# Attention operands on one core of a Trainium2: the bf16 parts stored once in DRAM and loaded by pairs of products, in place of six products stored and loaded whole

## The chip, the cores and the metric

The kernel runs on one core of one Trainium2 chip. The metric is the time on the device in microseconds, the median of several executions. Three executions of the kernel before gave 1299.5, 1299.62 and 1301.71 us.

## The reference

Eight blocks run over one sequence of 2048 tokens of width 128, each with a layer norm before it and a residual after it: softmax attention, channel mix, gated linear attention, channel mix, retention, mixture of experts, lightning attention, mixture of experts. Only the first one matters here:

```python
def attention(x, W_qkv, q_scale, k_scale, W_out):          # 16 heads of 8, causal
    q, k, v = split(x @ W_qkv)
    q, k = layernorm(q) * q_scale, layernorm(k) * k_scale   # over all 128 channels
    s = einsum('bshd,bthd->bhst', q / sqrt(8), k)
    s = where(future, finfo.min, s)
    return einsum('bhst,bthd->bshd', softmax(s), v).reshape(B, S, D) @ W_out
```

## The kernel before

Tokens are handled in 4 chunks of 512. The scores are needed in float32, while the two operands of their matmuls are bf16. So each of q and k is split into three bf16 parts, high, mid and low, and the score is the sum of six products of parts (`PRODUCTS`: high·high, mid·high, low·high, high·mid, mid·mid, high·low). A head has 8 channels, so six products make 48 rows; three more rows (`extra`) hold the row maximum of q, split in the same way, against ones in k. These 51 rows (`KROWS`) are the contraction of every score matmul. Heads are paired: one of a pair has partitions 0 to 50 ("side" 0), the other partitions 64 to 114 (side 1). `Qs` and `Ks` are the resident stacks in SBUF, laid out [partition, pair, 2048 tokens] in bf16.

There are two blocks of code; no engine starts the second one before all are done with the first.

The first block loads x and all the weights on SP's queue (lines 387 to 404), normalises, projects to q, k, v, normalises q and k, turns them (line 546), and splits them into parts (`take_high`, `take_rest`, `take_mid`, `take_low`). The parts of a chunk are `parts[c]`, [128 partitions, q or k, 3 parts, 512 tokens]. A partition of it is (side, channel, pair), while a partition of the stack is (side, product, channel), with all eight pairs in it. So the parts pass through DRAM. `store(c)` (line 369) writes them with 12 DMAs into two DRAM tensors `q_stack` and `k_stack`, where each of the 6 products is written out in full, in rows of 1 KB. `stack(c)` (line 377) waits for `stored[c]` and loads Qs and Ks with 4 DMAs, each 48 partitions of one side, in pieces of 1 KB: first Q and K of side 0, then Q and K of side 1. SP runs `store(0)`, `stack(0)`, `store(1)` at the end of the first block, and `stack(1)`, `store(2)`, `stack(2)`, `store(3)`, `stack(3)` in the second.

The second block is the attention. It goes through 16 steps, each of one group of 4 heads and one chunk of queries: (group 0, chunk 0), (1, 0), (0, 1), (1, 1), (0, 2) and so on. For each step there are a pass for the row maxima (score matmuls at line 765, causal mask at 754 and 755, DVE's reduction at 714), then the maxima split by GpSimd (692 to 695), turned by TensorE (810), copied by DVE to `mrow` (727) and put into the rows 48 to 50 of Qs by four small DMAs, one for each head of the group (`set_maxima`, line 653: on ACT's queue for the first four steps, on SP's queue after them). Then come the transposed scores (782), exp on ACT (827), the causal cut on GpSimd (684), and the product with the values (796). All engines follow one order that `attention_order` plans beforehand. In that order the first maxima of step 2 (chunk 1) stand right behind those of step 1, and the first transposed scores of step 0 (`scores`, which wait for `max_set[j]`) right behind the first maxima matmul of step 2. The maxima of steps 2 and 3 need `stacked[1]`; chunk 2 is first needed by step 4, after all the maxima of step 3. After the attention each stage waits for the one before it.

Of the kernel before, what the change touches and what calls it, by code (L numbers as in the profile page):

```python
# [5 lines left out]
BF16 = mybir.dt.bfloat16  # L6
# [8 lines left out]
HD = D // H  # L15
P = 128
NT = T // P
CH = 512
NC = T // CH
# [6 lines left out]

ST = TOP * NT + E - 1
PARTS = 3
PRODUCTS = [(0, 0), (1, 0), (2, 0), (0, 1), (1, 1), (0, 2)]
PAIRS = H // 2  # L30
MROW = len(PRODUCTS) * HD
KROWS = MROW + PARTS
# [27 lines left out]
def build(nc, io):  # L60
    ctx = ExitStack()
    with ctx:
        def sb(name, shape, dt=FP32):
            return ctx.enter_context(nc.sbuf_tensor(name, shape, dt))
# [3 lines left out]
        def sem(name):  # L68

            stage_sems.append(nc.alloc_semaphore(name=name))  # L70
            return stage_sems[-1]
# [28 lines left out]
        arena = sb("arena", [P, 24 * 1024 + 8])  # L100
# [8 lines left out]
        left, right, table = cstb[:, 0:P], cstb[:, P:2 * P], cstb[:, 2 * P:320]  # L109


        stacks = [nc.dram_tensor(name, [NC, 2, MROW, PAIRS * CH], BF16, kind="Internal").ap() for name in ("q_stack", "k_stack")]

# [180 lines left out]
        def softmax_attention():  # L296

            QK = PAIRS * T // 2
            Qs, Ks = (arena[:, i * QK:(i + 1) * QK].bitcast(BF16).rearrange("p (n t) -> p n t", n=PAIRS) for i in (0, 1))
            at = 2 * QK  # L300
            room = [arena[:, at + i * 3 * CH:at + (i + 1) * 3 * CH] for i in (0, 1)]
            room += [w2[:].rearrange("p e f d -> p (e f d)")[:, i * 3 * CH:(i + 1) * 3 * CH] for i in (0, 1)]
            parts = [r.bitcast(BF16).rearrange("p (s r t) -> p s r t", s=2, r=PARTS) for r in room]
# [9 lines left out]
            with ExitStack() as mem:  # L313
# [40 lines left out]
                stored = [sem(f"a_stored{c}") for c in range(NC)]  # L354
                stacked = [sem(f"a_stacked{c}") for c in range(NC)]

                def store(sp, c):

                    row = PAIRS * CH
                    for s in (0, 1):  # L360
                        r = 0
                        for n in (3, 2, 1):
                            for side in (0, 1):
                                half = slice(side * P // 2, (side + 1) * P // 2)
                                if s == 0:
                                    src = parts[c][half, s, 0:n, :]
                                else:
                                    src = parts[c][half, s, 3 - n:4 - n, :].to_broadcast([P // 2, n, CH])
                                sp.dma_start(bass.AP(tensor=stacks[s].tensor, offset=((c * 2 + side) * MROW + r * HD) * row,
                                                     ap=[[CH, P // 2], [HD * row, n], [1, CH]]), src).then_inc(stored[c], 16)  # L370
                            r += n

                def stack(sp, c):
                    sp.wait_ge(stored[c], 16 * 12)
                    for side in (0, 1):
                        for dst, src in ((Qs, stacks[0]), (Ks, stacks[1])):
                            sp.dma_start(dst[64 * side:64 * side + MROW, :, c * CH:(c + 1) * CH],
                                         src[c, side].rearrange("r (n t) -> r n t", n=PAIRS)).then_inc(stacked[c], 16)

                def small_x(i, c):  # L380
                    return small[:, i, c * TPC:(c + 1) * TPC]
# [1 line left out]
                with nc.Block() as block:  # L383
                    @block.sync
                    def _(sp):
                        for c in range(NC):
                            sp.dma_start(x[:, c * TPC:(c + 1) * TPC, :],
                                         io["x"].rearrange("a (t p) d -> p (a t) d", p=P)[:, c * TPC:(c + 1) * TPC, :]).then_inc(x_loaded[c], 16)
                            if c == 0:
                                sp.dma_start(cst[:], io["cst"]).then_inc(tables_loaded, 16)  # L390
                                sp.dma_start(w["qkv"][:], io["qkv"]).then_inc(qkv_loaded, 16)
                        sp.dma_start(masks32[:], io["masks"]).then_inc(masks_loaded, 16)
                        for i, name in enumerate(("q_scale", "k_scale")):
                            sp.dma_start(scale[:, i:i + 1], io[name].rearrange("(n a) -> n a", a=1)).then_inc(scales_loaded, 16)
                        for i in (0, 1):
                            for side in (0, 1):
                                row = 64 * side + MROW
                                sp.dma_start(arena[row:row + PARTS, i * QK:(i + 1) * QK], io["extra"][i]).then_inc(extra_loaded, 16)
                        for name, _ in WEIGHTS[1:]:
                            sp.dma_start(w[name][:], io[name]).then_inc(loaded, 16)  # L400
                        sp.dma_start(w["lg2"][:], io["lg2"]).then_inc(loaded, 16)
                        sp.dma_start(out_bias[:], io["out_b"].rearrange("(a n) -> a n", a=1).to_broadcast([P, D])).then_inc(loaded, 16)
                        for i, name in enumerate(VECTORS):
                            sp.dma_start(vec[:, i:i + 1], io[name].rearrange("(n a) -> n a", a=1)).then_inc(loaded, 16)

                        sp.wait_ge(extra_loaded, 64)
                        for c in (0, 1):
                            sp.wait_ge(low, 2 * (c + 1))
                            store(sp, c)
                            if c == 0:  # L410
                                stack(sp, c)
# [236 lines left out]
                def set_maxima(eng, k):  # L648
                    g, c = STEPS[k]
                    eng.wait_ge(ring_read, RING["turn max", k] + 1)  # L650
                    for j in range(GH):
                        row = 64 * (j % 2) + MROW
                        eng.dma_start(Qs[row:row + PARTS, 2 * g + j // 2, c * CH:(c + 1) * CH],
                                      mrow[j * P // GH:j * P // GH + PARTS * TPC, :]).then_inc(max_set[j], 16)

                with nc.Block() as block:
                    @block.sync
                    def _(sp):
                        stack(sp, 1)
                        for c in (2, 3):  # L660
                            store(sp, c)
                            stack(sp, c)
                        for k in range(EARLY, NS):
                            set_maxima(sp, k)
                        for j in range(GH):
                            sp.wait_ge(max_set[j], 16 * NS)
                        sp.wait_ge(loaded, 16 * LOADS)
# [72 lines left out]
                    def _(pe):  # L740
                        def free_slot(what, n):

                            m = RING[what, n]
                            if m >= 2:
                                pe.wait_ge(ring_read, m - 1)
                            return RB + 2 * (m % 2)

                        def rows(stack, side, pair, a, z):
                            return stack[64 * side:64 * side + KROWS, pair, a:z]

                        def add_mask(side, out):

                            half = slice(64 * side, 64 * side + 64)
                            nc.tensor.matmul(out[:, 0:64], left[half], table[half], start=False, stop=False)
                            return nc.tensor.matmul(out[:, 64:P], right[half], table[half], start=False, stop=True)

                        def scores_for_max(n):

                            k, t, pl, kc, width = MAXIMA[n]
                            g, c = STEPS[k]  # L760
                            if n == m0[k]:
                                pe.wait_ge(stacked[c], 64)
                            bank = free_slot("max", n)
                            for side in (0, 1):
                                ins = nc.tensor.matmul(ps[:, bank + side, 0:width],  # L765
                                                       rows(Qs, side, 2 * g + pl, (c * TPC + t) * P, (c * TPC + t + 1) * P),
                                                       rows(Ks, side, 2 * g + pl, kc * CH, kc * CH + width), start=True, stop=kc < c)
                            if kc == c:
                                for side in (0, 1):
                                    ins = add_mask(side, ps[:, bank + side, width - P:width])  # L770
                            ins.then_inc(ring_ready, 1)
# [616 lines left out]
        def experts(name, token_rows, result_rows, last):  # L1388
# [54 lines left out]
            with nc.Block() as block:  # L1443
# [223 lines left out]
                def _(pe):  # L1667
# [37 lines left out]
                    for i in range(ST + 2):  # L1705
# [19 lines left out]
                        if s >= 0:  # L1725
# [6 lines left out]
                            ins.then_inc(down_ready, 1)  # L1732

        softmax_attention()
        channel_mix("f0")
        linear_attention("g", "gated")
# [77 lines left out]
```

## Time and profile before

| | |
|---|---|
| profiled execution, its own time | 1301.57 us |
| its span | 1299.8 us |
| TensorE matmul busy | 994.5 us |
| VectorE busy | 903.7 us |
| ScalarE busy | 508.2 us |
| GpSimd busy | 400.1 us |
| HBM read, written | 37.94 MB, 16.91 MB |
| packets of SP's DMA queue (q1) | 47480, 44.78 MB |

Busy time is the time in which an engine works on an instruction; DMA-issuing instructions are not in it. A DMA is issued by an engine's queue (SPq, ACTq) in about half a microsecond, and its data moves later on 16 DMA engines; a packet is one contiguous piece. In views of windows the DMA share can be over 1, because a packet's whole time is put down to the window in which it starts. The chain that ended last, as the page gives it, reaches back only to 1119 us and lies in the last mixture of experts, so it says nothing on the part that is changed; that part is at 28 to 100 us.

### The profile page before, as it was taken

The page shows a single profiled execution, that of the slowest core. Times are in us where ns is not written, and L with a number is a line of the kernel's source. Part 1 is how long each engine was busy: PE and PEld are TensorE (multiplying, and loading weights), DVE is VectorE, ACT ScalarE, POOL GpSimd, SP SyncE. Part 2 cuts the span into 40 slices and gives each one's busy share as a digit, 9 for nine tenths or more (in the row PEclk, how much of TensorE's full clock was granted, in tenths as well). Part 3 has the DMA queues.
Part 4 walks back from the last instruction along what each step waited for, and adds up shares of the span by engine and source line. Part 5 has one row for each costly group of instructions (what it writes and reads, how often), then busy time and mean ns, then how long its engine had stood idle before and what let it go on. Part 6 is the DMA issues. An engine that isn't in the chain of part 4 may idle for free. (4 is left out here: it accounts for less than half of the span.)

```text
span 1299.8 us, 17329 instructions
## 1 busy us (share of the span) xinstructions
PE 994.5 (77%) x5802; PEld 497.3 (38%) x5802; DVE 903.7 (70%) x1529; ACT 508.2 (39%) x1042; POOL 400.1 (31%) x479
## 2 busy tenths in 40 slices
PE   5477898999999998686667665399975775459994
PEld 3222222222222313444553213166652444336663
DVE  6957889898898700889977996633347997653335
ACT  5244566787778665321021001033334211113333
POOL 3211111011111112254434442156643444226662
PEclk9557789899999976789768985599997986669997
DMA  5890000000000001412101211011122120101114
GB/s 131 174 189 13 2 1 1 1 2 2 2 1 2 2 2 36 158 58 73 33 1 41 65 40 33 12 34 44 42 55 81 35 63 8 33 17 43 42 43 114
DMA packets 52797, 56.16 MB, mean 43 GB/s; under 512 B 7957, under 2 KB 40093, under 8 KB 52701
## 3 DMA queue, kind: packets, MB, share of 16 engines
q1 hardware_dynamic: 47480, 44.78, 13.5%
q0 software_dynamic: 4992, 10.23, 2.9%
q8 instruction: 50, 0.82, 0.3%
q14 instruction: 35, 0.28, 0.1%
q10 hardware_dynamic: 240, 0.05, 0.0%
HBM read 37.94 MB, written 16.91 MB: 42 GB/s over the span
## 5 line engine op out<-in xcount | busy, mean ns | idle before, releaser
L714 DVE TENSOR_REDUCE mpart<-ps 128x2 f32<-128x1024 f32 (+3 forms) x320 | 325.2, 1060 | 63.0 <-PE ps L765 38.3
L827 ACT ACTIVATE arena<-ps 128x512 f32<-128x512 f32 (+3 forms) x640 | 292.5, 541 | 155.1 <-PE ps L782 145.7
L782 PE MATMUL ps<-arena 51*128 51x512 bf16 (+3 forms) x640 | 187.5, 386 | 17.0 <-ACT arena L827 8.8
L1057 POOL TENSOR_TENSOR arena<-arena 128x512 f32<-128x512 f32 x96 | 122.2, 1273 | 165.1 <-DVE arena L1110 163.3
L796 PE MATMUL ps<-arena,w 128*32 128x512 f32 (+3 forms) x1280 | 168.9, 603 | 4.6 <-ACT arena L827 3.7
L765 PE MATMUL ps<-arena 51*128 51x512 bf16 (+3 forms) x640 | 152.0, 388 | 23.3 <-DVE mpart L714 15.3
L684 POOL TENSOR_SCALAR_AFFINE_SELECT arena<-arena 128x512 f32<-128x512 f32 x64 | 40.6, 635 | 325.8 <-ACT arena L827 254.3
L1559 DVE COPY arena<-ps 128x128 f32<-128x128 f32 x78 | 22.8, 292 | 161.7 <-PE ps L1702 161.7
L1649 ACT ACTIVATE arena<-ps 128x512 f32<-128x512 f32 x78 | 46.6, 597 | 218.9 <-PE ps L1712 218.9
L782 PEld LDWEIGHTS ps<-arena 51*128 51x128 bf16 x640 | 50.3, 96 | 186.7 <-ACT arena L827 146.4
L1096 DVE TENSOR_TENSOR arena<-arena 128x512 f32<-128x512 f32 x62 | 102.0, 1645 | 12.3 <-ACT arena L1163 4.6
L1614 POOL DMA_INDIRECT results<-arena x78 | 76.8, 984 | 90.5 <-DVE arena L1576 90.5
L1603 POOL DMA_INDIRECT arena<-tokens,arena x78 | 75.7, 970 | 76.9 <-DVE arena L1552 53.7
L1110 DVE TENSOR_TENSOR_SCAN arena<-cst,arena 128x512 f32<-128x512 f32 x64 | 87.4, 1366 | 0.0
L1711 PE MATMUL ps<-w,arena 128*128 x156 | 82.3, 610 | 2.9 <-DVE arena L1559 2.9
L1730 PE MATMUL ps<-w,arena 128*128 x624 | 82.7, 275 | 1.2 <-DVE arena L1576 1.2
L1712 PE MATMUL ps<-w,arena 128*128 x156 | 81.2, 603 | 0.0
L1730 PEld LDWEIGHTS ps<-w,arena 128*128 128x128 f32 x624 | 75.8, 192 | 1.6 <-issue 1.5
L182 PE MATMUL ps<-cst,xn 128*128 128x128 f32 x96 | 22.2, 393 | 60.5 <-DVE xn L165 58.7
L189 ACT COPY xt<-ps 128x512 f32<-128x512 f32 x28 | 16.2, 589 | 126.9 <-PE ps L182 126.9
L765 PEld LDWEIGHTS ps<-arena 51*128 51x128 bf16 x640 | 37.5, 97 | 69.3 <-DVE mpart L714 47.2
L1207 PE MATMUL ps<-arena 128*128 128x128 f32 x256 | 44.0, 326 | 25.9 <-POOL arena L1057 25.8
(261 smaller groups left out, 1479.6 us busy)
## 6 DMA issues: line engine op xcount, KB each, us to landing
w<-in_w SPq DMA_DIRECT2D x2, 2048.0 KB, 10.8
arena<-results SPq DMA_DIRECT2D x16, 256.0 KB, 5.1
arena<-g_v SPq DMA_DIRECT2D x15, 256.0 KB, 3.6
arena<-r_v SPq DMA_DIRECT2D x15, 256.0 KB, 3.6
arena<-l_v SPq DMA_DIRECT2D x15, 256.0 KB, 3.6
arena<-q_stack SPq DMA_DIRECT2D x8, 384.0 KB, 7.0
arena<-k_stack SPq DMA_DIRECT2D x8, 384.0 KB, 8.9
tokens<-arena SPq DMA_DIRECT2D x8, 256.0 KB, 2.4
```

The source lines that it names most:

```text
L714: nc.vector.tensor_reduce(out=mpart[:, 2 * pl:2 * pl + 2, t, kc], in_=ps[:, bank:bank + 2, 0:width], axis=AX.X, op=ALU.max).then_inc(ring_ ...
L765: ins = nc.tensor.matmul(ps[:, bank + side, 0:width], rows(Qs, side, 2 * g + pl, (c * TPC + t) * P, (c * TPC + t + 1) * P), rows(Ks, side, ...
L782: nc.tensor.matmul(ps[:, n % ST, off:CH], rows(Ks, j % 2, 2 * g + j // 2, kt * P, (kt + 1) * P), rows(Qs, j % 2, 2 * g + j // 2, c * CH + ...
L796: ins = nc.tensor.matmul(ps[32 * j:32 * j + 32, O, off:CH], vg[kt // (NT // 2)][:, kt % (NT // 2), g * GH + j, :], probs[:, u % 2, j, off: ...
L827: nc.scalar.activation(probs[:, n % 2, j[0], off:CH], ps[:, (GH * n + j[0]) % ST, off:CH], ACT.Exp, scale=float(HD) ** -0.5).then_inc(exp_ ...
L1057: nc.gpsimd.tensor_tensor(z[:, n % ZB, :], state[:, n % SB, :], q[:, c % 2, :], ALU.mult).then_inc(z_ready, 1)
L1096: nc.vector.tensor_tensor(upd[:, n % 2, :], v_in, k[:, n // HD % 2, :], ALU.mult).then_inc(upd_ready, 1)
L1110: nc.vector.tensor_tensor_scan(out=state[:, n % SB, :], data0=a, data1=upd[:, n % 2, :], initial=0.0 if c == 0 else state[:, (n - HD) % SB ...
L1614: nc.gpsimd.indirect_dma_start(out=result_rows, out_offset=bass.IndirectOffsetOnAxis(ap=result_row[:, s:s + 1], axis=0), in_=y[:, s % YB, ...
L1711: nc.tensor.matmul(ps[:, i % 2, :], xsT[:, i % 2, :], w1[:, expert[i], :], start=True, stop=True)
L1712: nc.tensor.matmul(ps[:, 2 + i % 2, :], xsT[:, i % 2, :], w3[:, expert[i], :], start=True, stop=True).then_inc(up_ready, 1)
L1730: ins = nc.tensor.matmul(ps[:, 7, 0:D], hidT[:, s % 2, f, :], w2[:, expert[s], f, :], start=f == 0, stop=f == NF - 1)
```

## The change

`store(c)` becomes one DMA: the three parts of q and k go to a DRAM tensor `sources` once each, 768 rows of 1 KB. `stack(c)` becomes 12 DMAs: for each pair of products (rows n and n+1 of `PRODUCTS`), each side, and each of Q and K, one DMA fills 16 partitions with 8 KB each. For that the products are put into another order (so that the two of a pair are a fixed distance apart in `sources`, which may be zero), and the resident stacks are laid out [partition, chunk, pair, 512 tokens], so that a partition's 8 pairs of a chunk are contiguous, in SBUF and in DRAM. The matmuls read the same values in rows as long as before.

```diff
-PRODUCTS = [(0, 0), (1, 0), (2, 0), (0, 1), (1, 1), (0, 2)]
+PRODUCTS = [(0, 0), (2, 0), (1, 0), (1, 1), (0, 1), (0, 2)]
...
-        stacks = [nc.dram_tensor(name, [NC, 2, MROW, PAIRS * CH], BF16, kind="Internal").ap() for name in ("q_stack", "k_stack")]
+        sources = nc.dram_tensor("sources", [NC, 2, PARTS, P, CH], BF16, kind="Internal").ap()
...
-            Qs, Ks = (arena[:, i * QK:(i + 1) * QK].bitcast(BF16).rearrange("p (n t) -> p n t", n=PAIRS) for i in (0, 1))
+            Qs, Ks = (arena[:, i * QK:(i + 1) * QK].bitcast(BF16).rearrange("p (c n t) -> p c n t", c=NC, n=PAIRS) for i in (0, 1))
...
                 def store(sp, c):
-                    row = PAIRS * CH
-                    for s in (0, 1):
-                        r = 0
-                        for n in (3, 2, 1):
-                            for side in (0, 1):
...
-                                sp.dma_start(bass.AP(tensor=stacks[s].tensor, offset=((c * 2 + side) * MROW + r * HD) * row,
-                                                     ap=[[CH, P // 2], [HD * row, n], [1, CH]]), src).then_inc(stored[c], 16)
-                            r += n
+                    sp.dma_start(sources[c].rearrange("s r p t -> p (s r) t"),
+                                 parts[c].rearrange("p s r t -> p (s r) t")).then_inc(stored[c], 16)
 
                 def stack(sp, c):
-                    sp.wait_ge(stored[c], 16 * 12)
-                    for side in (0, 1):
-                        for dst, src in ((Qs, stacks[0]), (Ks, stacks[1])):
-                            sp.dma_start(dst[64 * side:64 * side + MROW, :, c * CH:(c + 1) * CH],
-                                         src[c, side].rearrange("r (n t) -> r n t", n=PAIRS)).then_inc(stacked[c], 16)
+                    sp.wait_ge(stored[c], 16)
+                    for n in range(0, len(PRODUCTS), 2):
+                        for side in (0, 1):
+                            for s, stack_of in enumerate((Qs, Ks)):
+                                first, second = PRODUCTS[n][s], PRODUCTS[n + 1][s]
+                                row = 64 * side + n * HD
+                                at = ((c * 2 + s) * PARTS + first) * P * CH + side * P // 2 * CH
+                                sp.dma_start(stack_of[row:row + 2 * HD, c].rearrange("r n t -> r (n t)"),
+                                             bass.AP(tensor=sources.tensor, offset=at, ap=[[(second - first) * P * CH, 2], [PAIRS * CH, HD],
+                                                                                           [1, PAIRS * CH]])).then_inc(stacked[c], 16)
...
-                        eng.dma_start(Qs[row:row + PARTS, 2 * g + j // 2, c * CH:(c + 1) * CH],
+                        eng.dma_start(Qs[row:row + PARTS, c, 2 * g + j // 2, :],
...
-                            return stack[64 * side:64 * side + KROWS, pair, a:z]
+                            return stack[64 * side:64 * side + KROWS, a // CH, pair, a % CH:a % CH + z - a]
...
-                                pe.wait_ge(stacked[c], 64)
+                                pe.wait_ge(stacked[c], 16 * 12)
```

## Rows read from the trace of the kernel before

**Rows 1.** The page: busy time by engine, and TensorE's granted clock in 40 slices.
```profile
PE 994.5 (77%) x5802; PEld 497.3 (38%) x5802; DVE 903.7 (70%) x1529; ACT 508.2 (39%) x1042; POOL 400.1 (31%) x479
PEclk9557789899999976789768985599997986669997
```

**Rows 2.** The page: the costliest group, the reduction of the row maxima.
```profile
L714 DVE TENSOR_REDUCE mpart<-ps 128x2 f32<-128x1024 f32 (+3 forms) x320 | 325.2, 1060 | 63.0 <-PE ps L765 38.3
```

**Rows 3.** Windows (stretch: its length, busy time of five engines, PEclk, DMA share, GB/s).
```profile
140.00:460.00 320.00, 295.62 (x2383) 91.65 (x2379) 277.22 (x303) 230.85 (x491) 32.47 (x84) 0.94 0.01 2
```

**Rows 4.** Waits, 50 to 100 us (total, times, longest, in us).
```profile
PE ps L782 <- DMA arena<-mrow: 3.8, 2, 2.7
...
PE ps L765 <- DMA arena<-k_stack: 2.4, 1, 2.4
```

**Rows 5.** Timeline of PE (start, length, line, operation; in brackets the idle time before).
```profile
67.46 0.61 PE L765 MATMUL ps<-arena 51*128 51x512 bf16 x2 [2.40 <-DMA arena<-k_stack]
69.09 1.29 PE L782 MATMUL ps<-arena 51*128 51x512 bf16 x3 [1.02 <-DMA arena<-mrow]
...
84.76 1.21 PE L782 MATMUL ps<-arena 51*128 51x512 bf16 x3 [2.74 <-DMA arena<-mrow]
```

**Rows 6.** Timeline of SP's queue: stores (L369) and loads (L377) of the chunks.
```profile
28.98 3.99 SPq L369 DMA_DIRECT2D q_stack<-arena  x6
...
38.38 0.64 SPq L377 DMA_DIRECT2D arena<-q_stack  x1
...
41.05 3.89 SPq L369 DMA_DIRECT2D q_stack<-arena  x6
...
54.76 0.58 SPq L377 DMA_DIRECT2D arena<-q_stack  x1
...
71.45 0.58 SPq L377 DMA_DIRECT2D arena<-q_stack  x1
...
74.06 3.92 SPq L369 DMA_DIRECT2D q_stack<-w  x6
```

**Rows 7.** Windows around the transfers, columns as in rows 3.
```profile
4.00:8.00 4.00, 0.00 (x0) 0.00 (x0) 1.66 (x11) 0.59 (x2) 1.23 (x2) 1.00 1.04 341
...
39.50:50.00 10.50, 4.08 (x16) 2.99 (x16) 10.37 (x22) 4.48 (x7) 2.76 (x3) 0.50 1.05 158
50.50:54.00 3.50, 1.45 (x24) 1.04 (x24) 2.38 (x5) 0.40 (x1) 0.00 (x0) 0.50 1.07 370
57.00:66.00 9.00, 4.78 (x55) 2.42 (x51) 7.95 (x12) 0.00 (x0) 0.83 (x4) 0.50 1.12 165
...
75.00:83.50 8.50, 5.48 (x41) 1.76 (x40) 3.87 (x5) 2.14 (x8) 1.27 (x2) 0.50 1.11 151
...
516.00:523.00 7.00, 6.71 (x45) 6.30 (x43) 4.01 (x13) 2.35 (x4) 0.00 (x0) 0.77 0.97 335
```

**Rows 8.** Window of half a microsecond, halfway through the load of chunk 0.
```profile
45.00:45.50 0.50, 0.11 (x1) 0.00 (x0) 0.50 (x3) 0.35 (x1) 0.00 (x0) 0.50 1.06 211
```

**Rows 9.** DMA view: issue of the extra rows; then the packets of 9-10 and 18-20.5 us.
```profile
arena<-in_extra SPq DMA_DIRECT2D x4, 96.0 KB
...
DMA packets 403, 0.24 MB, mean 242 GB/s; under 512 B 163, under 2 KB 400, under 8 KB 400
...
DMA packets 470, 0.31 MB, mean 124 GB/s; under 512 B 55, under 2 KB 467, under 8 KB 467
```

**Rows 10.** Timeline of SP's queue: two issues that took ten times their usual 0.43 us.
```profile
11.73 4.64 SPq L400 DMA_DIRECT2D w_rq<-in_rq  x1
...
18.79 4.58 SPq L400 DMA_DIRECT2D w_lv<-in_lv  x1
```

**Rows 11.** Timeline of DVE: its last instruction of the first block.
```profile
50.16 1.46 DVE L488 TENSOR_TENSOR w<-arena,w 128x512 bf16<-128x512 f32 x2
```

**Rows 12.** Timeline of ACT's queue: the maxima of steps 0 and 1 sent to Qs.
```profile
62.77 3.90 ACTq L653 DMA_DIRECT2D arena<-mrow  x4
...
75.40 3.06 ACTq L653 DMA_DIRECT2D arena<-mrow  x4
```

More of the change, by code:

```diff
@@ L357, in store @@
                 def store(sp, c):
-                    row = PAIRS * CH
-                    for s in (0, 1):
-                        r = 0
-                        for n in (3, 2, 1):
-                            for side in (0, 1):
[L364 to L368, printed above, removed]
-                                sp.dma_start(bass.AP(tensor=stacks[s].tensor, offset=((c * 2 + side) * MROW + r * HD) * row,
-                                                     ap=[[CH, P // 2], [HD * row, n], [1, CH]]), src).then_inc(stored[c], 16)
-                            r += n
-                def stack(sp, c):
-                    sp.wait_ge(stored[c], 16 * 12)
-                    for side in (0, 1):
-                        for dst, src in ((Qs, stacks[0]), (Ks, stacks[1])):
-                            sp.dma_start(dst[64 * side:64 * side + MROW, :, c * CH:(c + 1) * CH],
-                                         src[c, side].rearrange("r (n t) -> r n t", n=PAIRS)).then_inc(stacked[c], 16)
+                    sp.dma_start(sources[c].rearrange("s r p t -> p (s r) t"),
+                                 parts[c].rearrange("p s r t -> p (s r) t")).then_inc(stored[c], 16)
+                def stack(sp, c):
+                    sp.wait_ge(stored[c], 16)
[8 more added lines that the diff above has]
+                                                                                           [1, PAIRS * CH]])).then_inc(stacked[c], 16)
                 def small_x(i, c):
```

## The prediction

> **What bounds the kernel now.** First the page's busy times [rows 1]: TensorE 994.5 us, VectorE 903.7 us of a span of 1299.8; the reader sees that neither is full all the time, and that the granted clock changes between its two levels, 1.2 and 2.4 GHz. The largest group is the reduction of the maxima, 320 times 1060 ns [rows 2]. The windows [rows 3] then show that from 140 us to the end of the attention TensorE is busy in 296 and VectorE in 277 of 320 us, with the DMA engines idle (share 0.01): this stretch is limited by computing, and in a fixed order. Nothing in it depends on a transfer of the chunks, so a delay or a gain at its start goes through to the end unchanged. The change can be worth only what transfers cost before 100 us. The waits there [rows 4] name two: 2.4 us for `k_stack`, and 3.8 us for `mrow`, the maxima on their way to Qs. The timeline of PE [rows 5] places them: at 67.46 the first maxima of chunk 1 start after the wait for the loaded stack; at 69.09 and at 84.76 the transposed scores of steps 0 and 1 start after waits for the maxima. These are the three places to work out. The last view is SP's queue [rows 6] beside the windows [rows 7].
>
> **How the transfers run before.** A chunk moves 1.57 MB out (12 stores) and 1.57 MB in (4 loads). The windows [rows 7] show two speeds: stretches with only stores go at 370 GB/s (50.5 to 54), stretches of loads at 151 to 165 (75 to 83.5 with hardly anything else: 151). So a load takes 1.57 / 0.151 = 10.4 us, and a store 4.3. The load of chunk 1 is issued at 54.76 [rows 6] and PE goes on at 67.46 [rows 5]: 12.7 us, so 2.3 us besides the data, of which I put 1.4 ahead of the first byte and 0.9 behind the last.
>
> The small DMAs of the maxima behave as if they stood in one line with everything SP has issued. The first of step 1 is issued at 75.40 [rows 12]; SP had by then issued the whole load of chunk 2 (from 71.45) and two stores (from 74.06) [rows 6]. That load's data ends at about 83.5 (71.45 + 1.4 + 10.4), and the maxima land at 84.76. Those of step 0, issued from 62.77, land at 69.09, when nearly all of the stores of chunk 2 are through. So their landing is set by the end of the data ahead of them.
>
> **What the change does to one store.** 12 issues (7.9 us from 28.98; SP goes on at 38.38, so 9.4 us in all [rows 6]) become one of some 0.6 us with 0.79 MB: 2.1 us at 370 GB/s, and 1.5 us around it as before: 4.2 us. The sure part is -5.2 us on each store that is waited for.
>
> **What it does to one load.** The bytes stay 1.57 MB; 4 issues become 12, at 0.62 us each 7.4 us, which hides behind the data unless that goes faster than 210 GB/s. The open cost is the speed. Row length explains nothing: 128 partitions get 341 GB/s at 4 to 8 us, where most rows are the 512 B of x, and 335 at 516 us with 2 KB rows [rows 7]; 1 KB stores get 370. What is different in the slow loads is that 48 neighbouring partitions of one side are written. The other case of few partitions is `in_extra`: 4 DMAs of 96 KB, each 3 partitions, sides in turn. The views [rows 9] show 3 packets of 8 KB or more starting at 9 to 10 us and again at 18 to 20.5 (four such triples in all, one a DMA), and SP's second long issue ends at 23.37 [rows 10]. 393 KB in 14.2 us is 27.7 GB/s, although the sides alternate. So 3 partitions get 28, 48 get 151, 128 get 340. The new loads write 16. Between 3 and 48 lie four doublings for 123 GB/s, 31 each; 16 is 2.4 doublings up: 102 GB/s. Against that, the speed rises for half a microsecond where the load passes from side 0 to side 1 (211 GB/s [rows 8]); the new order passes five times in place of one. 5 x 0.5 us at some 160 (0.4 MB) and the rest, 1.17 MB, at 102 make 2.5 + 11.5 = 14.0 us; I take 14.2. Bounds: 85 GB/s (18.5 us, towards a straight line between the two rows, which gives 63) and 210 (7.5 us, the issue).
> The Trainium skill (SBUF — State Buffer, Door 1: The DMA port swizzle) says that the partition number picks one of 16 ports: 16 neighbours reach 4 of them, 48 reach 8 with half of these carrying double. By its 27.2 GB/s a port the new loads get an estimated 109 GB/s, 14.4 us, and the sum below would be +3.3 in place of +3. By that rule 48 partitions would get 163 (the trace has 151), and 3 would get 27.2 (the trace has 27.7).
>
> **The sum, in order of time.** Chunk 0: store issued 28.98 as before (SP sends weights until then), landed 33.1; load issued 33.1, data 34.5 to 48.7 (before: to 50.2). Nothing is gained at the start of the attention: VectorE's last instruction of the first block ends at 51.62 [rows 11], and all wait for that; the stack of chunk 0 has landed 2 us before. Store 1 is issued at about 40.5, behind the load; its data is through at 50.8. So SP issues stack 1 at 51.9, when the block starts, not at 54.76: 2.9 us earlier. It takes 14.2 + 2.3 = 16.5 us: 68.4 against 67.46, **+0.9** (-2.9 + 3.8). Store 2 follows: data to 69.5. The maxima of step 0 have only it ahead: about 69.9 against 69.09, **+0.8** in all; ACT's four issues took 3.90 us beside SP's and 3.06 the next time [rows 12]; that 0.8 us gains nothing, since landing decides. SP sees store 2 landed at 69.8 (before 71.45) and issues stack 2: data 71.2 to 85.4, then store 3, issued at 77.2, to 87.5. The maxima of step 1 are issued from 76.2 to 79.3: the first has the load ahead and lands at 86, the other three have store 3 ahead too and land at 88. Against 84.76 that is +1.2 to +3.2; the first three are used at once, so **+3**. Load 3, issued at 88, is through by 104, before the maxima of step 2 are needed: nothing more. The matmuls read rows of the same length in the new layout, and the order of products costs nothing. After that there is no cover left to lose.
> Profiled: 1301.57 + 3 = 1304.6. The median of the runs shown lies 2 us under the profiled execution, so for the median 1299.6 + 3 = **1302.6**.
>
> **Rivals.**
> A rate per DMA engine. The 3 partitions of the extra rows may have used three DMA engines, 9.2 GB/s each; the 48 partitions used all 16, 151 / 16 = 9.4 each. If that is the limit for few partitions, or if the engines drift apart so that both sides are in use, 16 partitions get about 150 GB/s and a load stays at 10.4. Then stack 1 lands at 51.9 + 12.7 = 64.6: the wait of 2.4 us is gone; maxima of step 0 at 66.3 (-2.8); stack 2 issued at 66.3, data to 78.1, maxima of step 1 at 80.5: -4.2, **1295.4**. For it: the two equal quotients. Against it: 128 partitions give each engine 21, also with rows of one partition.
> Long rows are fast. Loads run as fast as they are issued, 210 GB/s: all three waits go, 3.6 us at the first two together and 2.7 us at the third: -6.3, **1293.3**. Against it: row length shows no effect in [rows 7]. The Trainium skill (Perfetto Trace Analysis, DMA Optimizations) has this rule, from 2 KB to 4 or 8 KB a great gain; no load of this trace bears it out.
> The two cancel: load of 12.3 to 13.5 us (117 to 128 GB/s, six passes between sides helping more than I allowed): stack 1 within 1 us of before, maxima of step 1 at 83.5 to 86: -1.3 to +1, **1299.6**.
> Slower on the other side of my forecast's range: the limit is sharper, as at 25 GB/s for the busiest sixth of a 48-partition load (151 / 6); four such make 100, or down to 85: load 15.7 to 18.5 us. Stack 1 lands at 70 to 73 (+2.6 to +5.5), stack 2's data ends at 88.5 to 94: +5.5 to +9, **1306**. It decides from 113 GB/s downwards: above that the earlier issue wins, below it the slower load.
>
> **Chances.** My forecast, slower loads at 102 to 113 GB/s, +1 to +4.5 us: 0.38. Sharper limit: 0.12. Cancel: 0.19. Rate per engine or drift: 0.24. Long rows: 0.07. What spreads each case further is the clock: it stays at 1.2 GHz through the transfers (0.50 [rows 7]) and is at 0.94 of full speed on the mean after 140 us [rows 3], so a shift of a few us can move the rise, which I put at one or two us either way. What can be told from no change is 0.2%, 2.6 us. Slower by more: two thirds of the forecast, all of the sharper limit, 0.02 of the cancelling: 0.39. Faster by more: 0.24 x 0.85, the long rows, and 0.03 of the cancelling: 0.30. The rest, 0.31, within. The range with 8 in 10: 1294.4 to 1306.6; the forecast's own is 1300.5 to 1304.5.
>
> **What would show it.** One SP issue at 28.98, the first of 12 loads at about 33; loads in windows without stores at 100 to 113 GB/s with DMA share at or over 1; stack 1 issued at 51.9 (sure: else SP was held up) and PE's first wait for `stacked` ending at 68 to 69; the scores of step 1 starting at 87 to 88. If the window of a load shows 150 or more, the forecast is wrong in its main term, and the end comes 4 us earlier than before; if PE waits less and the end is still not earlier, the clock or the order of the attention took it back.

## The result and the profile after

| | median | executions | span of the profiled one |
|---|---|---|---|
| before | 1300.61 us | 1299.5 to 1301.71 | 1299.8 us |
| after | 1333.96 us | 1328.55 to 1335.49 | 1326.8 us (its own time 1328.55) |

The ratio is 1.0243, with a 95% interval of 1.0206 to 1.0279: 2.4% slower. One further execution of the changed kernel took 1854 us, at a granted clock of 1.0; it is left out of the range and the ratio but not of the median, which is 1332.43 us without it, and nothing here explains it. The forecast was 1302.6 us, its range ended at 1306.6.

The page of the kernel after, for [rows 1] and [rows 2], and its list of waits from 30 to 200 us, for [rows 4]:

```profile
PE 989.6 (75%) x5802; PEld 497.5 (37%) x5802; DVE 904.1 (68%) x1529; ACT 508.6 (38%) x1042; POOL 400.2 (30%) x479
...
L709 DVE TENSOR_REDUCE mpart<-ps 128x2 f32<-128x1024 f32 (+3 forms) x320 | 325.2, 1060 | 93.9 <-PE ps L760 58.7
```
```profile
PE ps L760 <- DMA arena<-sources: 38.0, 2, 21.8
...
PE ps L777 <- DMA arena<-mrow: 3.2, 4, 1.2
```

The work is the same: 5802 matmuls, VectorE at 904.1 us against 903.7. (TensorE's 989.6 against 994.5 us goes with a higher granted clock at the end of the attention, below.) What has grown is waiting. PE waited 2.4 us for the stacks, now 38.0 in two pieces. PE's timeline, first in the kernel before, where the attention starts, then in the kernel after, against [rows 5] too:

```profile
51.94 0.29 PE L765 MATMUL ps<-arena 51*128 51x128 bf16 x2 [3.20 <-PEq L383]
```

```profile
64.64 0.29 PE L760 MATMUL ps<-arena 51*128 51x128 bf16 x2 [16.21 <-DMA arena<-sources]
...
99.60 0.60 PE L760 MATMUL ps<-arena 51*128 51x512 bf16 x2 [21.82 <-DMA arena<-sources]
100.00 1.06 PE L777 MATMUL ps<-arena 51*128 51x512 bf16 x3
...
115.07 0.60 PE L777 MATMUL ps<-arena 51*128 51x512 bf16 x1 [0.71 <-DMA arena<-mrow]
```

The attention starts at 64.6 us where it started at 51.9, and chunk 1 comes at 99.6 where it came at 67.5: +12.7, then +32.1 (both are differences of the rows shown). SP's queue, against [rows 6]:

```profile
28.56 0.38 SPq L359 DMA_DIRECT2D sources<-arena  x1
32.20 9.24 SPq L371 DMA_DIRECT2D arena<-sources  x12
41.48 2.08 SPq L359 DMA_DIRECT2D sources<-arena  x1
66.66 7.60 SPq L371 DMA_DIRECT2D arena<-sources  x12
```

The store is as short as hoped: 3.6 us from its issue to the first load. The load is not: issued at 32.20, it releases PE at 64.64. The windows give the reason, against [rows 7] (the last two columns are the DMA share and GB/s):

```profile
44.00:46.00 2.00, 0.81 (x4) 0.40 (x2) 2.00 (x8) 1.19 (x2) 0.00 (x0) 0.50 1.01 369
...
52.00:64.00 12.00, 0.00 (x0) 0.00 (x0) 0.00 (x0) 0.00 (x0) 0.00 (x0) 0.50 0.13 55
64.00:66.60 2.60, 1.44 (x24) 1.01 (x24) 1.24 (x3) 0.00 (x0) 0.00 (x0) 0.50 0.11 38
...
82.00:98.00 16.00, 0.00 (x0) 0.00 (x0) 0.00 (x0) 0.00 (x0) 0.00 (x0) 0.50 0.13 53
```

Loads go at 53 GB/s with a DMA share of 0.13, which is 2 engines of 16, each at 26.5. The share tells this from the limit that was forecast: with all engines held up at the destination it would be near 1, as it was before at 151 GB/s. In the windows from 52 and from 82 us no compute engine does anything. The store of chunk 1, issued behind the load, moves at 369 GB/s in the middle of it (44 to 46 us), as 14 engines would be free for it. SP sees it landed only at 66.66, 2 us behind the load: from 64.0 to 66.6 another 0.1 MB goes at 38 GB/s, which is 2/16 of the store's 0.79 MB. It fits that the two slow engines' part of the store came last; the windows do not name the engines.

From step 5 on the lag is constant. The copy of the maxima of step 5, and the one of the last step, in the kernel before and then in the kernel after (DVE's timeline):

```profile
189.56 0.21 DVE L727 COPY mrow<-ps 128x128 bf16<-128x128 bf16 x1
...
456.98 0.22 DVE L727 COPY mrow<-ps 128x128 bf16<-128x128 bf16 x1
```
```profile
219.76 0.21 DVE L722 COPY mrow<-ps 128x128 bf16<-128x128 bf16 x1
...
487.35 0.22 DVE L722 COPY mrow<-ps 128x128 bf16<-128x128 bf16 x1
```

+30.2 and +30.4 us. The span grew by 27.0; the other 3.4 came back at the end of the attention, where the granted clock was higher (last section).

### The profile page after: what moved, and what is told of

It is laid out like the page before. It is cut to its first block and busy times, and to the rows that moved or that the text cites. A ratio compares the mean times of both kernels' runs of the same rounds, so it can differ in the third digit from the quotient of the medians.

```text
span 1326.8 us, 17317 instructions
## 1 busy us (share of the span) xinstructions
PE 989.6 (75%) x5802; PEld 497.5 (37%) x5802; DVE 904.1 (68%) x1529; ACT 508.6 (38%) x1042; POOL 400.2 (30%) x479
## 5 line engine op out<-in xcount | busy, mean ns | idle before, releaser
L791 PE MATMUL ps<-arena,w 128*32 128x512 f32 (+3 forms) x1280 | 164.4, 588 | 5.0 <-ACT arena L822 4.0
```

Of the source, the lines that this page charges most:

```text
L791: ins = nc.tensor.matmul(ps[32 * j:32 * j + 32, O, off:CH], vg[kt // (NT // 2)][:, kt % (NT // 2), g * GH + j, :], probs[:, u % 2, j, off: ...
```

## The experiments

Theory E: a load runs on as many DMA engines as the outermost dimension of its DRAM side has entries; the change made that 2. Rival Z: 8 KB rows, the repeated reading of the same parts, or the single store are slow. Theory P is the prediction's: writing few neighbouring partitions limits a load. Theory L: the maxima's small DMAs stand in line behind the data issued before them. The labels that begin with e test the first three, those with v test L and loads over 128 partitions. All ratios are to the kernel before, run beside them.

**e1_channel_outer**: the changed kernel, channels outermost.

```diff
-    bass.AP(tensor=sources.tensor, offset=at, ap=[[(second - first) * P * CH, 2], [PAIRS * CH, HD], [1, PAIRS * CH]])
+    bass.AP(tensor=sources.tensor, offset=at, ap=[[PAIRS * CH, HD], [(second - first) * P * CH, 2], [1, PAIRS * CH]])
```

> The changed kernel, with one edit: in the 12 loads of a chunk the DRAM side's pattern has the 8 channels outermost and the 2 products inside, in place of 2 products outermost (the rows of a pair lie in the stack in another order, the same in Q and K). Bytes, rows of 8 KB, destinations and number of issues are the same. Theory E (a load runs only on as many DMA engines as the outermost dimension of its DRAM side has entries: 2 in the changed kernel, whose loads go at 53 GB/s with a DMA share of 0.13; here 8): the share rises to about 0.5, the speed at least twofold. If nothing else limits, 8 x 26.5 = 210 GB/s, a load of 7.5 us, and all waits for transfers go: 1294 us. Theory E with the prediction's limit for 16 neighbouring partitions (102 to 110 GB/s): a load of 14.2 to 15.5 us, 1302 to 1306 us. Rival Z (rows of 8 KB, or parts read again from the same DRAM rows, are slow by themselves): 53 GB/s and 1332 us as in the changed kernel.

Measured: 1299.32 us against 1299.51, ratio 0.9993 (0.997 to 1.0016). The whole loss is gone by the order of two dimensions. The time is 3 us under what was expected of E with a limit for 16 partitions. The loads themselves took what the prediction gave them: PE goes on with chunk 1 16.5 us after the issue at 52.27.

```profile
52.31 0.29 PE L760 MATMUL ps<-arena 51*128 51x128 bf16 x2 [3.20 <-PEq L378]
...
68.76 0.61 PE L760 MATMUL ps<-arena 51*128 51x512 bf16 x2 [3.34 <-DMA arena<-sources]
...
82.48 0.61 PE L777 MATMUL ps<-arena 51*128 51x512 bf16 x1 [0.18 <-DMA arena<-mrow]
```

A window with nothing but the load of chunk 2 on the DMA engines:

```profile
72.00:79.00 7.00, 5.47 (x34) 1.47 (x31) 3.23 (x5) 2.18 (x6) 2.02 (x6) 0.66 0.51 118
```

Share 0.51: 8 engines, 118 GB/s, not 8 x 26.5 = 212. Z falls, since the rows, the repeated reading and the single store are all still there, and a second limit shows.

**e2_one_product**: one product, 8 partitions, in each load.

```diff
-    for n in range(0, len(PRODUCTS), 2):
+    for n in range(len(PRODUCTS)):
...
-    sp.dma_start(stack_of[row:row + 2 * HD, c]..., ap=[[(second - first) * P * CH, 2], [PAIRS * CH, HD], [1, PAIRS * CH]])
+    sp.dma_start(stack_of[row:row + HD, c]..., ap=[[PAIRS * CH, HD], [1, PAIRS * CH]])
```

> The changed kernel with each load taking one product in place of two: 24 loads a chunk, each 8 partitions of 8 KB, the DRAM side's outermost dimension 8 (the channels). Theory E alone: 8 DMA engines, up to 210 GB/s, so limited by 24 issues of 0.62 us, 15 us a chunk: 1302 to 1306 us, windows of loads at about 105 GB/s. Theory E with the limit by neighbouring partitions (27 GB/s for each four of them): 8 partitions get 50 to 55 GB/s although 8 engines work, share about 0.5 with little moved, a load of 29 us: 1330 us, as slow as the changed kernel. Rival Z: 53 GB/s and 1332 us too, but with a DMA share near 0.13.

Measured: 1334.05 us, ratio 1.0252 (1.0198 to 1.0305). The window shows the second limit alone:

```profile
72.00:82.00 10.00, 0.00 (x0) 0.00 (x0) 0.96 (x2) 0.00 (x0) 0.00 (x0) 0.50 0.53 66
```

Share 0.53, so 8 engines as in e1, but 66 GB/s on 8 partitions where e1 has 118 on 16. As slow as the change, for another reason; the share tells the two apart. (PE waits 24.4 us for stacks here and another 20.4 us for maxima.)

**e3_rows_8k_48**: the kernel before with only the new layout, so 4 loads of 48 rows of 8 KB.

```diff
-    sp.dma_start(dst[64 * side:64 * side + MROW, :, c * CH:(c + 1) * CH], src[c, side].rearrange("r (n t) -> r n t", n=PAIRS))
+    sp.dma_start(dst[64 * side:64 * side + MROW, c].rearrange("r n t -> r (n t)"), src[c, side])
```

> The kernel before (12 stores of all six products, 4 loads of 48 partitions), with only the new layout of the resident stacks, so that each load moves rows of 8 KB in place of 1 KB on 16 DMA engines. Theory of the prediction (few neighbouring partitions limit, row length doesn't): loads at 150 to 165 GB/s as before, 1299.6 us within 1.5. Rival, long rows are fast: loads at 210 GB/s or more, 7.5 us or less, all waits for transfers go: 1293 to 1295 us.

Measured: 1300.01 us, ratio 0.9981 (0.9952 to 1.001).

```profile
41.00:49.00 8.00, 4.08 (x16) 3.00 (x16) 7.94 (x21) 3.91 (x6) 0.83 (x1) 0.50 1.01 148
```

148 GB/s; before it is 153 in the same window. Rows of 8 KB bring nothing.

**e4_16_rows_16_engines**: e3 with 12 loads of 16 rows that lie one after another in DRAM.

```diff
-    for side in (0, 1):
+    for n in range(0, MROW, 16):
+        for side in (0, 1):
...
-            sp.dma_start(dst[64 * side:64 * side + MROW, c]..., src[c, side])
+                sp.dma_start(dst[64 * side + n:64 * side + n + 16, c]..., src[c, side, n:n + 16])
```

> The kernel before with its 12 stores and DRAM stacks, the new layout of the resident stacks, and 12 loads of 16 partitions x 8 KB a chunk: the shape and destinations of the changed kernel's loads, but each reads 16 rows one after another in DRAM (outermost dimension 16). Theory E with the prediction's limit for 16 partitions: 102 to 110 GB/s with all 16 engines busy (share about 1), a load of 14.4 to 15.4 us in place of 10.4; the attention starts 3.6 us later, the maxima of step 1 land some 12 us later: 1309 to 1314 us. Theory E alone: 16 engines, limited by the issue at 210 GB/s: 1294 to 1297 us.

Measured: 1305.32 us, ratio 1.004 (1.0018 to 1.0062), 4 us under the expected range: a load ran at 120 and not at 106, and the attention started at 52.5 us and not 3.6 us late.

```profile
40.00:50.00 10.00, 4.08 (x16) 3.00 (x16) 9.87 (x22) 4.24 (x7) 2.52 (x2) 0.50 1.04 120
```

16 engines are busy (1.04) and move 120 GB/s, as 8 did in e1 with 118. On 16 partitions the number of engines beyond 8 doesn't matter.

**e5_outer_2** and **e6_outer_4**: e3, the load's 48 rows written as 2 x 24, and as 4 x 12.

```diff
-    src[c, side]
+    bass.AP(tensor=src.tensor, offset=(c * 2 + side) * MROW * PAIRS * CH,
+            ap=[[MROW // 2 * PAIRS * CH, 2], [PAIRS * CH, MROW // 2], [1, PAIRS * CH]])
```

> The kernel of e3_rows_8k_48 (12 stores of all products, 4 loads of 48 partitions x 8 KB), with the DRAM side of each load written as 2 x 24 rows in place of 48 rows: the same bytes from the same addresses to the same partitions. Theory E (engines = outermost dimension of the DRAM side): 2 engines, DMA share 0.13, 53 GB/s, a load of 30 us in place of 10.4, as in the changed kernel; the attention starts at about 70 us and waits again for chunk 1: 1333 to 1345 us. Rival (the single store, the repeated reading of parts, or 16-partition pieces made the changed kernel slow): loads at 150 GB/s, 1300 us.

> As e5_outer_2, with 4 x 12 rows. Theory E: 4 engines, DMA share 0.25, 4 x 26.5 = 106 GB/s, a load of 14.8 us; the attention starts about 4 us later and waits more for chunk 1 and the maxima, near e4_16_rows_16_engines: 1304 to 1312 us. Rival: 150 GB/s, 1300 us.

Measured: 1299.96 and 1293.31 us, ratios 0.9997 (0.9962 to 1.0033) and 0.9977 (0.9938 to 1.0016); their loads ran at about 150 GB/s with shares near 1 (e5 152 GB/s at 0.99 from 41 to 49 us, e6 151 at 0.98 from 76 to 82). Both expectations missed: the dimensions lie end to end in memory, so the pattern names one run of rows, and it was treated as one. They tested nothing of E, and led to e7.

**e7_outer_2_gap**: e5 with an unused row between the halves in DRAM, which the stores skip.

```diff
-    [NC, 2, MROW, PAIRS * CH]
+    [NC, 2, MROW + 2, PAIRS * CH]
...
-    ap=[[MROW // 2 * PAIRS * CH, 2], ...]
+    ap=[[(MROW // 2 + 1) * PAIRS * CH, 2], ...]
```

> The kernel of e3_rows_8k_48 with one unused row left in the DRAM stacks between rows 23 and 24 of each side, so that the DRAM side of a load is 2 x 24 rows that can't be merged into 48. (In e5 and e6 the two dimensions lay end to end, and the windows show 16 engines still working: the form was merged, so they tested nothing.) Same bytes, partitions, rows of 8 KB and number of DMAs. Theory E: 2 engines, share 0.13, 53 GB/s, 30 us a load: the attention starts near 70 us and waits again for chunk 1: 1333 to 1345 us. Rival (single store, repeated reading or 16-row pieces made the changed kernel slow): 150 GB/s, 1300 us.

Measured: 1341.91 us, ratio 1.0325 (1.0274 to 1.0376). PE's timeline:

```profile
70.88 0.29 PE L766 MATMUL ps<-arena 51*128 51x128 bf16 x2 [22.21 <-PEq L384]
...
106.77 0.61 PE L766 MATMUL ps<-arena 51*128 51x512 bf16 x2 [22.77 <-DMA arena<-k_stack]
```

And a window early in the load of chunk 0:

```profile
42.00:44.00 2.00, 1.09 (x5) 0.79 (x6) 2.00 (x9) 0.00 (x0) 0.20 (x1) 0.50 0.14 57
```

Share 0.14 at 57 GB/s, two engines again; later windows also hold pieces of the store. The load of chunk 0 is issued at 37.15, so PE starts 33.7 us after it, as in the change (32.4). (SP needs 21 us for the six issues of stores behind that load, where it needed 3.9 [rows 6].) The attention starts at 70.9, as expected. The stores are those of before but for the skipped row, each row of DRAM is read once, and the loads have 48 partitions: besides the rows of 8 KB, which e3 cleared, the one thing shared with the change is the outermost 2. With e1, which takes it away, and e7, which brings it alone, E is shown for 2.

**v3_before_gated**: the kernel before with waits on SP, so that the maxima have nothing ahead of them.

```diff
-    for c in (2, 3):
-        store(sp, c)
-        stack(sp, c)
+    sp.wait_ge(max_set[GH - 1], 16)
+    store(sp, 2)
+    sp.wait_ge(max_set[GH - 1], 32)
+    stack(sp, 2)
+    store(sp, 3)
+    sp.wait_ge(max_set[GH - 1], 48)
+    stack(sp, 3)
```

> The kernel before with only the order on SP changed: the store of chunk 2 is issued after the maxima of step 0 have landed, the load of chunk 2 and the store of chunk 3 after those of step 1, the load of chunk 3 after those of step 2. Theory L (the small DMAs of the maxima land only when the data issued ahead of them is through): PE goes on at 67.5 with the maxima of chunk 1 as before, the scores of step 0 start at about 67.9 in place of 69.1, those of step 1 without a wait, 4 us earlier in all: 1295 to 1296.5 us. Rival (the maxima take their time by themselves, or the order of the attention gives the time back): within 1 us of before, with the wait at the scores of step 1 still there.

Measured: 1295.47 us against 1300.08, ratio 0.9969 (0.9942 to 0.9997). From 50 to 100 us PE has 2.9 us of waits for stacks, as before, and none for the maxima; only a weight load waits 0.3 us for them:

```profile
PE ps L769 <- DMA arena<-k_stack: 2.9, 1, 2.9
PEld ps L786 <- DMA arena<-mrow: 0.3, 1, 0.3
```

L holds: 3.8 us of waits [rows 4] were only a place in line. The trace says it more firmly than the ratio, whose interval nearly reaches 1: at the last copy of the maxima the kernel is at 453.05 us where before it is at 456.98, 3.9 earlier.

**v4_channel_outer_gated**: e1 with the same order on SP.

> The kernel of e1_channel_outer (parts stored once, loads of 16 partitions on 8 DMA engines) with the same order on SP as v3_before_gated. Theory L: the stack of chunk 1 lands at 68.8 as in e1, the scores of step 0 start at 69.2, those of step 1 without the waits of 1.2 us in all: 1297 to 1298.5 us, 1 to 2 us under e1. If the single store is worth more than the slower load when nothing stands in line, it comes near v3_before_gated (1295.5).

Measured: 1297.53 us, ratio 0.998 (0.9959 to 1.0001): as expected, and not distinguishable from before, nor from v3, whose median is 2 us lower. That the single store makes up for 16-partition loads is not shown, and neither is the opposite.

**v2_loads_128**: e3 with DRAM stacks of 64 rows a side, filled once at the start in rows 48 to 63, and one load for all 128 partitions of Q and one for K.

```diff
-    for side in (0, 1):
-        for dst, src in ((Qs, stacks[0]), (Ks, stacks[1])):
-            sp.dma_start(dst[64 * side:64 * side + MROW, c].rearrange("r n t -> r (n t)"), src[c, side])
+    for dst, src in ((Qs, stacks[0]), (Ks, stacks[1])):
+        sp.dma_start(dst[:, c].rearrange("r n t -> r (n t)"), src[c].rearrange("a r m -> (a r) m"))
```

> The kernel before with 12 stores, the new layout of the resident stacks, and DRAM stacks of 64 rows a side, whose rows 48 to 63 are filled once at the start (zeros for q, ones for k), so that a chunk is loaded with 2 DMAs over all 128 partitions, 8 KB each. A load moves 2.1 MB in place of 1.57. Theory P (the speed of a load goes by the partitions it writes): 340 to 375 GB/s, 5.7 us of data; the stack of chunk 1 is issued at 51.9, landed at 60, and its wait goes; the maxima of step 0 stand behind the load of chunk 2 and land at 69 to 70 as before; those of step 1 at 80.5, before they are needed: 1296.5 to 1298 us. Rival (a load of the stacks is limited to 150 GB/s by something else, such as DRAM pages or 16 rows of 8 KB in flight): 14 us of data, slower than before, 1302 to 1306 us.

Measured: 1300.61 us, ratio 0.9994 (0.9967 to 1.002), 3 us over the expectation. Its loads are fast, but the fill and the extra rows hold SP up at the start, which I had left out:

```profile
37.07 3.96 SPq L370 DMA_DIRECT2D q_stack<-arena  x6
```
```profile
57.50 0.29 PE L767 MATMUL ps<-arena 51*128 51x128 bf16 x2 [8.60 <-PEq L382]
```

The first store is issued 8 us later than before (28.98 [rows 6]), and the attention starts at 57.5, 5.6 us late. What the loads gave, the start took.

**v6_loads_128_no_extra**: v2 without the four loads of the extra rows into SBUF (they come with the chunks).

```diff
-    for side in (0, 1):
-        row = 64 * side + MROW
-        sp.dma_start(arena[row:row + PARTS, i * QK:(i + 1) * QK], io["extra"][i])
```

> The kernel of v1_loads_128_gated with the order on SP of the kernel before (no wait for the maxima): it parts what the fast loads bring from what the order brings, and differs from v2_loads_128 only by the extra rows that are no longer loaded into SBUF (in v2 they and the fill of the DRAM rows held SP up, and the attention began at 57.5 us). Theories P and L: attention begins at 51.6 as in v1, no wait for the stack of chunk 1, the maxima of step 0 stand behind the load of chunk 2 and land at 68 to 69.5, those of step 1 behind chunk 3's data: 1294 to 1297 us, 2 to 4 us above v1. If the order is worth nothing once loads are fast: equal to v1.

Measured: 1296.26 us against 1300.24, ratio 0.9965 (0.9935 to 0.9995). **v1_loads_128_gated** is the same with `sp.wait_ge(max_set[GH - 1], 32)` ahead of the load of chunk 2.

> The kernel of v2_loads_128 without the loads of the extra rows into SBUF (they come with the chunks), and with the load of chunk 2, the store and the load of chunk 3 issued after the maxima of step 1 have landed. Theories P and L together: all three waits for transfers before 100 us go (2.4, then 1.2 and 2.7, and what hangs on them): the scores of step 0 start at about 65.9, those of step 1 at 78.5: 6 us earlier, 1293 to 1295 us. If the attention gives some back by waits among the engines: 1295 to 1297.

Measured: 1289.83 us against 1300.08, ratio 0.9949 (0.9919 to 0.9979), the lowest of all, and 3 us under the expectation. Its executions lie at 1286 to 1290 (six) and 1294 to 1297 us (five), so the 10 us between the medians overstate the gain. PE in v6, then the load of chunk 3 and PE's wait for maxima in v1:

```profile
70.50 0.60 PE L780 MATMUL ps<-arena 51*128 51x512 bf16 x2 [3.24 <-DMA arena<-mrow]
```
```profile
90.00:95.00 5.00, 2.34 (x19) 1.00 (x15) 4.61 (x8) 0.58 (x1) 0.83 (x4) 0.74 0.98 403
...
PE ps L782 <- DMA arena<-mrow: 0.2, 1, 0.2
```

The stacks of 128 partitions load at 403 GB/s, and no wait for a stack is left. v6 still has 3.2 us for maxima behind the load of chunk 2; in v1 the order takes it away. The intervals of the two ratios overlap, so the difference is read from the last copy of the maxima, first in v6, then in v1 (before: 456.98):

```profile
453.36 0.22 DVE L725 COPY mrow<-ps 128x128 bf16<-128x128 bf16 x1
```
```profile
450.64 0.22 DVE L727 COPY mrow<-ps 128x128 bf16<-128x128 bf16 x1
```

The fast loads are 3.6 us ahead of before, the order adds 2.7: 6.3 in all, as expected. The profiled execution of v1 is 14 us shorter than that of before; the other 7.5 us come in the stretch up to the load of `w1`, where its granted clock was higher (last section).

## Why the prediction was wrong

**What bounds the kernel; where a delay goes: right but for the clock.** The lag came through the attention nearly unchanged, 30.2 to 30.4 us over the last 268 us of it. Not all went through to the end: 3.4 us came back at the end of the attention, by the clock; the prediction allowed the clock "one or two us either way" for a shift of a few us.

**One store: right.** 3.6 us from issue to SP going on, against 4.2.

**One load: wrong, and this is the step that failed.** The term was "I take 14.2" us, at 102 GB/s, with a lower bound of 85 GB/s (18.5 us). I read the speed of a load from the partitions it writes and took for granted that all 16 DMA engines carry it, also where I wrote the rivals. The new loads' DRAM side is [2 products][8 channels][8 KB], so each runs on two engines: 53 GB/s, 29.7 us, twice the term. The sign that the prediction named, a DMA share at or over 1 in windows of loads, came out at 0.13. There was a hint beforehand, no more: `in_extra`, with 3 rows a DMA, had three long packets a DMA, so at most three engines carried each. I used it for the speed and named "three DMA engines" only in a rival, without asking what number the new loads would have. The Trainium skill has the rule (DMA: Bandwidth & Descriptors, Why a DMA increments its semaphore by 16 and not by 1): the number of engines is the largest up to 16 that divides the slowest dimension larger than 1 of both sides. For the change that gives 2, for e1 and e2 8, for e3 and e4 16, for e7 2; the shares of 0.13, 0.51 and 0.53, 1.01 and 1.04, and 0.14 agree with it.

**The sum around that term: right where it is put in.** With 29.7 in place of 14.2 the timetable gives chunk 0 at 32.2 + 2.3 + 29.7 = 64.2 (measured 64.64) and chunk 1 at 66.66 + 32.0 = 98.7 (99.60); 32.2 and 66.66 are the measured issues. Its line "Nothing is gained at the start of the attention" named 2 us of cover but no risk: the load of chunk 0 moved that start by 12.7 us.

**The forecast's mechanism, tried without that fault (e1): right in the load, wrong in the last term.** Loads of 16 partitions are slower than those of 48: 118 to 120 GB/s against 148 to 153. The estimate by doublings (102) was 14 to 15% under these windows, but the time was right: predicted for stack 1 were the issue at 51.9 and PE going on at 68.4, e1 has 52.27 and 68.76. The +3 us came from the maxima of step 1, which were to land at 86 to 88; in e1 PE takes them at 82.48 to 84.75, before was 84.76. They are issued at 75.96, when SP is 5.5 us into the 8.66 us that its 12 issues of that load take, so they would have only about two thirds of the load ahead of them, not all of it. Without that term earlier issue and slower load cancel, as the ratio of 0.9993 shows: the rival's time, though stack 1 came as in the forecast.

**The rivals.** "Long rows are fast" is refuted by e3. "A rate per DMA engine" of 9.4 GB/s is refuted by the change, where an engine moves 26.5, and by e2: 8 engines move 66 GB/s on 8 partitions and 118 on 16 (e1).

**The line of small DMAs: right** (v3, and v1 against v6).

## What to carry to other kernels

Before a DMA is reshaped, read both its patterns from the outside: the outermost dimension that doesn't merge with the next set the number of engines here, and in the windows the DMA share tells it (0.13 is two). Then ask how many partitions it writes, and divide the speed by the busy engines: in the change it was 26.5 GB/s an engine, and more engines helped; at 15 (e1), 8 (e2) or 9 (before) the engines were held up by something else, here the few partitions, whatever the share. And small transfers that someone waits for should be issued before the large ones that nobody needs yet; that order alone was worth 0.3% here (v3, 3.9 us by its trace).

## What the runs showed of the hardware

Speed of a load by the partitions of one DMA, with the engines at work:

| partitions | engines | GB/s | from |
|---|---|---|---|
| 8 | 8 | 66 | e2 |
| 16 | 8 and 16 | 118, 120 | e1, e4 |
| 48 | 16 | 148 to 153 | e3, before |
| 128 | 16 | 403 | v1 |

Each figure is one window with hardly anything but loads; other such windows give 62 to 76 in e2, 114 to 121 in e1 and 113 to 115 in e4. The size of a DMA grows with its partitions here (64, 128, 384 KB and 1 MB), and no run holds one and varies the other; against the size alone speaks `in_extra`, 96 KB a DMA on 3 partitions at the prediction's 27.7 GB/s. By the ports of the Trainium skill (SBUF — State Buffer, Door 1: The DMA port swizzle) an estimate gives 54, 109 and 163 for the first three rows; the order agrees, while the windows shown are 21% and 8 to 10% above it and then 6 to 9% below it. Stores read 64 partitions of one side at a time and yet reach 370 GB/s [rows 7]; the limit of the loads does not show in them.

The granted clock at the end of the attention differs between executions. e3 and e6 move the same bytes in the same way (e6's pattern was merged), yet the profiled ones have spans of 1299.4 and 1291.7 us. The same stretch, first in e3, then in e6:

```profile
460.00:500.00 40.00, 36.27 (x188) 7.67 (x188) 1.10 (x4) 25.23 (x62) 6.34 (x10) 0.66 0.00 1
```
```profile
460.00:500.00 40.00, 33.73 (x232) 9.45 (x228) 1.65 (x6) 29.80 (x76) 8.88 (x14) 0.92 0.00 1
```

At 0.92 in place of 0.66 TensorE does 232 matmuls and not 188 in these 40 us. At the last copy of the maxima e6 is 0.8 us ahead of e3; SP then issues the load of `w1`, which stands behind the attention, at 506.23 in e6 and at 514.58 in e3: 7.5 us of the 7.7 arise in this stretch. v1's profiled execution has 0.90 there, before has 0.66. In the changed kernel, with its lag of 30 us, it is 0.78 from 490.4 to 536 us; its load of `w1` is issued at 541.56, before's at 514.94, so of the lag of 30.4 us 3.8 went back there (3.4 by the end of the span). What decides the clock there stays open. A median of few executions can therefore be off by some microseconds, as e6's 1293.31 is; the intervals of the ratios contain that.
